# Two attention-and-FFN layers: value products by halves behind the quantized FFN, and the next layer's first query chunks by token halves

## The reference

```python
x = x + _L0_xattn_ref(_layernorm(x), ctx_1024, ctx_1024, Wq, bq, Wk, bk, Wv, bv, Wo, bo)   # 16 heads of 16
x = x + _L0_ffn_ref(_layernorm(x), w_gate, w_up, w_down)           # blockwise FP4 of inputs and hidden, silu(gate) * up
x = x + _L1_xattn_ref(_layernorm(x), ctx_1024, ctx_1024, mask, W_Q, W_K, W_V, W_O)         # 16 heads of 64, masked
x = x + _L1_ffn_ref(_layernorm(x), w1, b1, w2, b2)                 # fixed point, piecewise linear GELU
```

## Time and profile before

| | us |
|---|---|
| median of 3 runs | 946.16 (944.98 to 946.4) |
| profiled execution | 946.27 |
| span of the profiled execution | 944.5 |
| PE busy | 901.0 (95%) |
| DVE busy | 670.0 (71%) |
| ACT busy | 601.8 (64%) |
| POOL busy | 204.6 (22%) |

### The profile page before, as it was taken

How to read it: one execution, slowest core, us unless ns; L and a number is a source line. 1 busy time by engine, 2 the same in 40 slices (tenths; PEclk the granted TensorE clock), 3 DMA queues, 4 the chain that set the end, 5 groups by cost and what they waited for, 6 DMA issues and landing times.

```text
span 944.5 us, 16084 instructions
## 1 busy us (share of the span) xinstructions
PE 901.0 (95%) x5546; PEld 592.5 (63%) x5546; DVE 670.0 (71%) x2179; ACT 601.8 (64%) x1671; POOL 204.6 (22%) x316
## 2 busy tenths in 40 slices
PE   6899999999999999999999999999999999999998
PEld 2555574767656565577665566567756655647686
DVE  4999872763889785475598978267478988727558
ACT  3788425972779643695369943399257984259835
POOL 3211001772000000476000000077400000028500
PEclk9999999999999999999999999999999999999999
DMA  9500100000000010000000010000000000000000
GB/s 295 201 1 2 28 0 23 2 1 1 1 1 24 1 28 23 1 1 2 0 1 8 18 28 1 23 1 1 1 1 1 18 7 1 0 1 2 1 1 23
DMA packets 14560, 18.35 MB, mean 19 GB/s; under 512 B 3088, under 2 KB 11664, under 8 KB 14480
## 3 DMA queue, kind: packets, MB, share of 16 engines
q1 hardware_dynamic: 12288, 15.40, 5.0%
q10 hardware_dynamic: 2064, 1.91, 0.7%
q0 software_dynamic: 128, 0.01, 0.0%
HBM read 15.21 MB, written 2.10 MB: 18 GB/s over the span
## 4 chain that ended last, share of the span: by engine, by line
PE 71%; DVE 14%; ACT 10%; issue 3%; POOL 1%; DVEq 0%; POOLq 0%
PE bank L1236 29%; PE bank L1251 9%; PE bank L1483 6%; PE bank L1559 6%; PE bank L1463 5%; PE bank L1342 4%; ACT ring L671 4%; PE bank L1399 4%; DVE row_max L1043 3%; PE bank L1376 3%; ACT ring L712 2%; ACT ring L556 1%; PE bank L1415 1%; PE bank L1529 1%; PE bank L1244 1%
## 5 line engine op out<-in xcount | busy, mean ns | idle before, releaser
L463 POOL TENSOR_TENSOR rstd<-var_eps,minus_half 128x2 f32<-128x2 f32 x32 | 23.4, 734 | 543.1 <-DVE var_eps L881 543.1
L556 ACT ACTIVATE ring<-bank 128x512 f32<-128x512 f32 x224 | 123.4, 611 | 17.4 <-PE bank L1251 16.0
L481 POOL TENSOR_TENSOR ring<-ring,row_inv 128x256 f32<-128x256 f32 x192 | 112.1, 612 | 101.9 <-DVE row_inv L1138 101.9
L1251 PE MATMUL bank<-ident_s,ring 128*128 128x128 f32 x768 | 105.1, 279 | 4.9 <-POOL ring L481 2.3
L1251 PEld LDWEIGHTS bank<-ident_s,ring 128*128 128x128 f32 x768 | 82.6, 141 | 39.5 <-issue 17.4
L712 ACT ACTIVATE ring<-ring,row_max 128x256 f32<-128x256 f32 x192 | 95.1, 496 | 17.3 <-DVE row_max L1131 17.3
L671 ACT ACTIVATE ring<-bank,row_max 128x256 f32<-128x256 f32 x192 | 88.4, 494 | 3.9 <-DVE row_max L1043 3.9
L1131 DVE CUSTOM_DVE_ANT_0 ring<-bank,maskbias 128x256 f32<-128x256 f32 x192 | 70.7, 420 | 23.4 <-issue 23.4
L1043 DVE TENSOR_REDUCE row_max<-bank 128x2 f32<-128x512 f32 x128 | 79.4, 683 | 5.6 <-PE bank L1376 4.9
L1236 PE MATMUL bank<-wgu_s,act_s 128*128 128x352 f32 x256 | 78.4, 459 | 0.0
L1236 PE MATMUL bank<-ctxT_s,wk_s 128*128 128x512 f32 x160 | 75.6, 596 | 0.7 <-DVE v L1029 0.7
(11 more groups left out here) (186 smaller groups left out, 1693.5 us busy)
## 6 DMA issues: line engine op xcount, KB each, us to landing
x_s<-x SPq DMA_DIRECT2D x4, 512.0 KB, 3.9
ctxT_s<-ctxT SPq DMA_DIRECT2D x4, 512.0 KB, 3.7
w_s<-w SPq DMA_DIRECT2D x2, 1024.0 KB, 16.3
out<-act_s SPq DMA_DIRECT2D x16, 128.0 KB, 1.7
wk_s<-wk SPq DMA_DIRECT2D x1, 1024.0 KB, 13.6
wv_s<-wv SPq DMA_DIRECT2D x1, 1024.0 KB, 14.8
wq_s<-wq SPq DMA_DIRECT2D x1, 1024.0 KB, 16.4
wo_s<-wo SPq DMA_DIRECT2D x1, 1024.0 KB, 16.6
```

The costliest lines, as they stand in the source:

```text
L481: ins = pool.tensor_tensor(probs1[i % PRING1][:, a, :], probs1[i % PRING1][:, a, :], row_inv[:, i, a:a + 1].to_broadcast([P, SEQ]), ALU.mult)
L556: act.activation(probsT[u % TRING][:, :, :].rearrange("p a q -> p (a q)"), psum(at, key)[:], ACT.Copy).then_inc(drain(at, key), 1)
L1251: ins = pe.transpose(psum(at, key)[:, c * SEQ + a * P:c * SEQ + (a + 1) * P], tile[:, a, c * P:(c + 1) * P], ident_s[:])
```

## The change

Two of the value products are cut into halves of 256 columns, in one bank each. The product `VALUES_LATE[1]` now has its first half ahead of the down product of tile 2 and its second half behind it. `VALUES_LATE[2]` has its first half ahead of the down product of tile 3 and its second half behind the first transposes of normalized rows; `VALUES_LATE[3]` stays whole and follows it, ahead of the second transposes. The query products m = 0 and 1 (`HALF_QUERIES`) are issued for the first 256 tokens as soon as the first half of `xnT` is there, and for the other 256 behind the wait for its second half. ACT copies `("xT2", 0)` ahead of `VALUES_LATE[2]`, not behind it. Bank assignments and all other engines' orders are as they were.

```diff
+HALF_QUERIES = 2
@@ ACT
                 evacuate_values(at, *VALUES_LATE[1])
-                for h in range(HALVES):
-                    evacuate_values(at, *VALUES_LATE[2 + h])
-                    evacuate_xT(at, 2, h, xnT)
+                evacuate_xT(at, 2, 0, xnT)
+                for t, n in VALUES_LATE[2:]:
+                    evacuate_values(at, t, n)
+                evacuate_xT(at, 2, 1, xnT)
@@ PE
+            def values_half(at, t, n, half):
+
+                key, columns = ("v1", t, n), slice(SEQ * half, SEQ * (half + 1))
+                if half == 0:
+                    wait_free(at, key)
+                for c in range(KC):
+                    ins = pe.matmul(psum(at, key)[:, columns], ctxT_s[:, c, t * P:(t + 1) * P],
+                                    wv1_s[:, c, 512 * n + columns.start:512 * n + columns.stop], start=(c == 0), stop=(c == KC - 1))
+                if half == 1:
+                    ins.then_inc(fill(at, key), 1)
+
+            def layer1_query_half(at, m, half):
+
+                key, tokens = ("q1", m), slice(SEQ * half, SEQ * (half + 1))
+                if half == 0:
+                    wait_free(at, key)
+                for c in range(KC):
+                    ins = pe.matmul(psum(at, key)[:, tokens], wq1_s[:, c, m * P:(m + 1) * P], xnT[:, c, tokens], start=(c == 0), stop=(c == KC - 1))
+                if half == 1:
+                    ins.then_inc(fill(at, key), 1)
@@ PE, loop over t
+                    if t == TILES:
+                        values_half(at, *VALUES_LATE[1], 0)
                     if t == TILES + 1:
-                        values(at, *VALUES_LATE[1])
+                        values_half(at, *VALUES_LATE[2], 0)
                     if t >= 2:
...
+                    if t == TILES:
+                        values_half(at, *VALUES_LATE[1], 1)
                     if 1 <= t <= TILES:
...
                 for h in range(HALVES):
-                    values(at, *VALUES_LATE[2 + h])
                     pe.wait_ge(xn_ready, g * (4 * TILES) + 2 * TILES + 2 * h + 2)
                     transpose_xn(at, 2, h, xn)
+                    if h == 0:
+
+                        values_half(at, *VALUES_LATE[2], 1)
+                        values(at, *VALUES_LATE[3])
                 for h in range(HALVES):
+
                     pe.wait_ge(*is_drained(at, ("xT2", h)))
-                for m in range(PAIRS):
+                    for m in range(HALF_QUERIES):
+                        layer1_query_half(at, m, h)
+                for m in range(HALF_QUERIES, PAIRS):
                     product(at, ("q1", m), psum(at, ("q1", m))[:], [(wq1_s[:, c, m * P:(m + 1) * P], xnT[:, c, :]) for c in range(KC)])
```

## The result

The changed kernel takes 936.35 us (median of 4 runs, 935.87 to 937.88) against 946.08 us before (4 runs, 944.98 to 946.4): the ratio is 0.9896, 95% interval [0.9883, 0.9909]. The forecast was 936.9, in a range of 935.2 to 940.2. The span of the profiled execution went from 944.5 to 934.1 us.

A forecast was written before the change was run, and what follows sets the result against it. TensorE, 95% busy, was taken to bound the kernel, so only its standing could be won. Four groups at 2.36 us less 0.1 for splitting save 9.3: 946.27 becomes 936.97, stated as 936.9, range 935.2 to 940.2.

The forecast's parts named there:

- What bounds it: TensorE, busy 95% of the span; time is won only where it stands, 2.87 us in group 1's stretch.
- Price of a half: A 256-column half costs 0.86 us; four split products add 0.02 us a group, 0.1 in all.
- Steps 1 and 2: Value halves fill the waits before tile 2's down product and tile 3's transposes, leaving 0.09 and 0.12 us.
- hT3: The transposes of hidden tile 3 on TensorE, forecast to start as before, at 364.66 in group 1.
- d2: The down product of hidden tile 2, forecast to start as before and take 2.59 us.
- A2: Second half of value product `VALUES_LATE[1]`, behind tile 2's down product: 0.86 us, residue 0.12.
- Step 3: With a value half behind tile 3's transposes, tile 3's down product starts 0.76 us earlier, residue 0.09.
- d3: The down product of hidden tile 3, forecast to start at 366.33 instead of 367.09 and take 2.59 us.
- Step 4: Before the second transposes of normalized rows: the normalization chain is late next, by 0.15 us.
- Step 5: First query halves start right behind the last transposes, second halves don't wait (slack 0.8); queries start 2.35 us earlier.
- The sum: Over four groups, 4 x 2.36 - 0.1 = 9.3 us saved from 946.27, giving 936.97, stated as 936.9.
- The rule against it: Split products' added weight loads, 16 a group of 190 ns, would be exposed: 949.0 us, a rival given 4%.

The follow-up runs named there:

- last wait filled: Changed kernel with query chunk 0's first token half moved ahead of the last transposes and chunk 2 also in halves: 936.11 us, ratio 0.9897 to before.
- spread values only: Changed kernel with value products spread in halves as in the change but all query products whole: 941.02 us, ratio 0.9943 to before.

## Why the prediction was right

- **What bounds it** held: PE's standing in the one stretch was what this change could win (PE also stands elsewhere, and that was not tried). All three waits fell below what the table shows, and nothing was given back: from the scores of group 1 to hidden tile 2's transposes of group 2 it is 581.71 - 378.19 = 203.52 us, where it was 587.25 - 383.69 = 203.56. These two rows, of before and then of the changed kernel, close that distance:

```profile
587.25 0.82 PE L1529 MATMUL bank<-ident_s,ring 128*128 128x128 f32 x6
```

```profile
581.71 0.82 PE L1556 MATMUL bank<-ident_s,ring 128*128 128x128 f32 x6
```

- **Price of a half**, 0.02 us a group, was right: 16 query half matmuls take 372.95 - 369.49 = 3.46 (3.45 forecast), and with every product cut it was 8 ns a product against the 5 or 6 worked out.
- **Steps 1 and 2.** The down product still starts 357.94 - 356.33 = 1.61 behind the transposes (361.09 - 359.48), hT3 361.50 - 357.94 = 3.56 behind that (3.57 before). Both starts are as forecast. One residue is not: d2, too, takes 360.61 - 357.94 = 2.67 and not 2.59, so half A2 ends at about 361.47, 0.03 ahead of hT3 and not 0.12.
- **Step 3.** d3 starts 363.16 - 361.50 = 1.66 behind hT3, 1.67 forecast, 2.43 before: 0.77 earlier.
- **Step 4** was right in kind and slightly mis-sized: the wait for the normalized rows is the 0.15 foreseen, but d3 takes 365.83 - 363.16 = 2.67, not 2.59. A down product that PE had to wait for takes 0.08 more here; its row is 2.83 long where the one that was not waited for is 2.75. That the first matmul is the slow one is my reading of it, from its weight load, which waits too. I had charged such a surcharge to transposes alone. The same term lets A2 overrun by 0.12 in group 0, where I had 0.04 (hT3 is 3.53 behind d2, 3.41 before).
- **Step 5** was right: the second query halves wait for nothing.
- **The sum.** To the queries it is 2.30 in groups 1 to 3 where 2.35 was forecast. To the scores it is 2.35, since the first query product, waited for before, now is not, and loses that same 0.08 (378.19 - 369.49 = 8.70 against 8.75). Group 0 gains 2.23 to the queries, not 2.36 (from d2 at 132.66 to the queries at 144.12, 11.46, against 147.17 - 133.48 = 13.69 in the earlier trace rows). To the queries the four groups gain 3 x 2.30 + 2.23 = 9.13, so the forecast's 9.3, which was counted there, is met only 0.2 short; counted to the scores it is met within 0.1, by two small errors that cancel. That the measured median then lies 0.5 us from the forecast is in part luck, as single runs of one kernel scatter by 2 to 3 us. Of the 10.4 us by which the profiled spans differ, 0.78 come from the warm-up ahead of all work (below) and are not the change's; some 0.3 are spread over the rest in pieces of 0.04 to 0.12 that I did not follow.
- **The rule against it**, that a weight load overlaps a running matmul only in another row group (the Trainium skill, TensorE: Matmul & The Clock Gate, Part 3), does not hold in this kernel: 93.3 us of added full-height loads cost 1.0 us. The row decides.

## What to carry to other kernels

When an engine that is 95% busy stands in a few short waits, measure each from start to start, and cut the independent filler to the wait's length: with halves of products there the kernel gained 2.30 us a group up to the queries, with whole ones 1.59 (0.95 of either from the query halves), because here a filler that was too long pushed the chain that the next wait was for. Split a consumer's first products along the axis in which their input arrives, so that the last part's copy is covered by work on the first. Then ask what is late next: here the last 0.15 us wait could be filled too, which the trace shows and the timing no longer does.

## What the hardware showed besides

The opening, which of all versions only the one with every product halved touches, differs between executions by more than filling the last wait gains. First, the four warm-up matmuls (eight rows) start at 6.78 in each profile, and the first keys follow at 13.00 (before), 12.22 (changed), 11.70 (last wait filled). The rows of before and then of the changed kernel:

```profile
6.78 6.38 PE L1566 MATMUL bank<-v 128*128 128x512 f32 x8 [6.78 <-POOL two L453]
13.00 3.60 PE L1236 MATMUL bank<-ctxT_s,wk_s 128*128 128x512 f32 x8
```

```profile
6.78 5.60 PE L1599 MATMUL bank<-v 128*128 128x512 f32 x8 [6.78 <-POOL two L454]
12.22 3.60 PE L1238 MATMUL bank<-ctxT_s,wk_s 128*128 128x512 f32 x8
```

Eight matmuls of 512 columns take 6.22 and 5.44 us, where eight later ones take 3.43 (16.43 - 13.00, where before's next row starts). The granted clock reads 1.00 all through, but the timeline of the weight loads shows two paces. At first the loads stand 0.85 us apart and are 0.33 or 0.34 us long, then 0.43 apart and 0.19 long. That is the pace of the lower level (1.2 GHz) and then of the higher (2.4). By the spacing of these rows, before and changed, the one changes over near 12.2 and the other near 10.7 (estimates); 1.5 to 1.6 us less at half the pace is the 0.78 between them:

```profile
12.06 0.27 PEld L1566 LDWEIGHTS bank<-v 128*128 128x128 f32 x1 [0.52 <-issue]
12.57 0.19 PEld L1236 LDWEIGHTS bank<-ctxT_s,wk_s 128*128 128x128 f32 x1 [0.24 <-issue]
```

```profile
10.35 0.34 PEld L1599 LDWEIGHTS bank<-v 128*128 128x128 f32 x1 [0.52 <-issue]
10.93 0.19 PEld L1599 LDWEIGHTS bank<-v 128*128 128x128 f32 x1 [0.24 <-issue]
```

What sets the moment, no run here shows.

Second, the granted clock can fall behind two waits of 1.08 (1.07 in some profiles) and 1.84 us. These are windows over layer 0's first value products (columns as in the earlier trace rows), in the changed kernel's first profile and in its second:

```profile
24.35:28.07 3.72, 3.72 (x20) 2.96 (x16) 3.48 (x7) 3.31 (x14) 2.36 (x1) 1.00 1.03 395
```

```profile
24.58:29.99 5.41, 5.41 (x20) 4.14 (x16) 3.66 (x7) 4.27 (x17) 2.35 (x1) 0.68 1.05 381
```

The same 16 matmuls take 3.72 and 5.41 us; a mean of 0.68 is a stretch at 1.2 GHz and a stretch at 2.4. Both executions had the same two waits ahead of them, so the waits alone do not decide it. The fall costs 1.7 us in three of the ten profiles here (spread values only, one query chunk in halves, and the changed kernel run again) and is absent from the others. It probably makes much of the scatter of single runs: the four runs of the changed kernel in its second measurement took 936.02 and 936.03 us at a mean clock of 1.000, and 937.9 and 937.94 at 0.998. Of these four only the one of 937.94 was profiled.
